# Where VectorE does three things of the last block: a normalisation, a final addition with its statistics, and one wait of GpSimd

## The chip, the cores and the metric

The kernel is one program on one core of a Trainium2 chip. The core has five engines that run their own instruction lists and meet through semaphores: TensorE (PE in the profile; its weight loads are PEld), VectorE (DVE), ScalarE (ACT), GpSimd (POOL) and SyncE (SP), which issues the DMAs. The metric is the time of the program on the device in microseconds; the times below are of one kernel executed three times.

## The reference

Input is a tensor of 8 sequences x 512 tokens x 256 channels. Two layers of a larger model are applied (an attention with a small gating network, a mixture of experts with slots; then a retention-like attention). The last block, which the change touches, is a local attention transformer with two layers:

```python
def _layer(x, wqkv, qs, ksc, wo, lg, lb, w1, b1, w2, b2):
    h = shift_token(x)                      # half of the channels come from the token before
    q, k, v = to_heads(split(h @ wqkv))     # 8 heads of 64
    q, k = rotary_xpos(l2norm(q) * qs, l2norm(k) * ksc)
    x = x + local_attention(q, k, v) @ wo   # windows of 128 tokens, own and previous one
    h = shift_token(x)
    h = (h - h.mean(-1)) / sqrt(h.var(-1) + 1e-05) * lg + lb
    a, g = split(h @ w1 + b1)
    x = x + (a * gelu(g)) @ w2 + b2
```

Behind the second layer the block's input is added again and the sum is normalised over the channels; that is the output.

## The kernel before, in words

All eight sequences stay in on-chip memory. The last block is one software pipeline of 75 slots (`SLOTS4` = 76, counted from 1). A slot takes one tile of 128 tokens of one sequence through each stage of the attention: 64 tiles (8 sequences x 4 tiles x 2 layers). The MLP work of a whole sequence (`m` = 0 to 15: eight sequences, two layers; m = 8 to 15 are the second layer) is cut in pieces and dealt over the slots by the table `PARTS_MLP`: MLP m begins in slot 4m + 7, and every slot has four parts. In the code `r` or `slot - 4m - 7` counts from there.

Each engine has its own function for a slot, and the order of its lines is the order of the engine's queue. The pieces that matter here:

- **gate and lin** (TensorE line 2046 for 128x512 and 2050 for the last piece of 64 rows): two halves of the first MLP product, six pieces each. ScalarE turns a gate with Gelu (line 2157), VectorE adds the bias to a lin and multiplies the two (line 2324, semaphore `m_hid`).
- **hT** (line 2037): transposes of the normalised rows `hn`; they wait for `m_norm`.
- **down** (line 2024): the second product; VectorE adds it to x in pairs (line 2307, `m_xw`).
- **scores** (line 1949), four banks s0 to s3 in two groups of 16 matmuls; VectorE takes row maxima (line 2231) and so frees the banks (`t_max`).
- **weights** (line 1964), w0 to w3: transposes of the probabilities; VectorE copies w0 and w2 out (line 2284, `t_pTd`), ScalarE w1 and w3 (line 2137).
- **normalise** (helper line 2604, four instructions, one a tile): subtracts the mean and multiplies by the reciprocal root. It is called on `hn` (`vector4_shifted`, sets `m_norm`) and on the finished x.
- **statistics** (helper lines 2589 and 2592, four of each), and the reciprocal root on GpSimd (lines 2597 and 2599).
- **final addition** (line 2335): x plus the reloaded input `again`, for m = 8 to 14; m = 15 has its own ending, `vector4_finish`.
- **bias** on GpSimd (line 2412): adds b_2 to x, 1024 values a partition.

Four banks of the accumulator memory (3, 4, 6, 7) go round among the kinds q, k, lin, gate, hT, s, w and down, in the order in which the program uses them; before a use, `emptied4` waits until the use four places earlier has been read. In slot 44 the order is q, k, lin 5, s0, s1, s2, s3, lin 4, hT 0, w0 to w3; in slot 45 it ends with down, w0, w1, w2, w3, gate 0, gate 1.

```python
place = self.ring4.place[kind, m, index] - 4
kind, m, index = self.ring4.uses[place]
w.wait_ge(*{... "w": ("t_pTa" if index % 2 else "t_pTd", 2 * m + index // 2 + 1),
    ... "lin": ("m_hid", 6 * m + LIN_AT[index % len(LIN_AT)] + 1)}[kind])
```

Of the kernel before, what the change touches and what calls it, by code (L numbers as in the profile page):

```python
# [7 lines left out]
ALU = mybir.AluOpType  # L8
# [3 lines left out]
SEQS, TOKENS, CH = 8, 512, 256  # L12
TILES = TOKENS // P
# [4 lines left out]
def split(ap, *sizes):  # L18
    names = "abcd"[:len(sizes)]
    return ap.rearrange(f"p ({' '.join(names)}) -> p {' '.join(names)}", **dict(zip(names, sizes)))  # L20
# [8 lines left out]
def repeated(ap, count):  # L29
    return ap.unsqueeze(1).to_broadcast([ap.shape[0], count] + list(ap.shape[1:]))  # L30
# [1712 lines left out]
TILES4, MLPS = LAYERS * LAYER, LAYERS * SEQS  # L1743
MLP_FIRST, MLP_STEP = 7, 4
# [14 lines left out]
def mlp_pieces(slot, part):  # L1759

    found = []
    for since, kind, index in PARTS_MLP[(slot - MLP_FIRST) % MLP_STEP][part - 1]:
        m = (slot - MLP_FIRST - since) // MLP_STEP
        if m == MLPS - 1 and kind in ("shift", "hT"):
            continue
        if 0 <= m < (SEQS if kind == "back" else MLPS):
            found.append((m, kind, index))
    last = slot - MLP_STEP * (MLPS - 1) - MLP_FIRST
    if (last, part) == (2, 2):
        found[1:1] = [(MLPS - 1, "hT", 0), (MLPS - 1, "hT", 1)]  # L1770
    return found + [(MLPS - 1, kind, index) for kind, index in PARTS_LAST.get((last, part), ())]
# [12 lines left out]
class Block4:  # L1784
# [501 lines left out]
    def vector4_mlp(self, e, w, slot, part):  # L2286
        s, S, own = self.s, self.S, self.own1
        for m in range(MLPS):
            if m == MLPS - 1 and slot == MLP_STEP * m + MLP_FIRST + 1 and part == 3:
                self.vector4_shifted(e, w, m)  # L2290
        if part == 1:
            for m in range(SEQS, MLPS - 1):
                if slot == MLP_STEP * m + MLP_FIRST + 7:
                    w.wait_ge("f_rstd", m - SEQS + 1)
                    self.normalise(e, self.norm4[1], self.x_nat[:, m - SEQS], s["f_norm"])
        for m, kind, index in mlp_pieces(slot, part):
            l, b = divmod(m, SEQS)
            if kind == "down" and m == MLPS - 1:
                self.vector4_finish(e, w, m, index)
                continue  # L2300
            if kind == "down":
                if index % 2:
                    pair = index // 2
                    x = self.x_nat[:, b, 2 * pair:2 * pair + 2]
                    w.wait_ge("m_w2", 4 * m + index + 1)
                    w.wait_ge("m_bias", m + 1)
                    e.tensor_tensor(x, x, split(self.bank4("down", m, 2 * pair), 2, CH), ALU.add).then_inc(s["m_xw"], 1)
                continue
            if kind == "shift":
                w.wait_ge("m_half", 2 * m + 2)  # L2310
                self.stats_of(e, w, "m_shifted", [32 * (m + 1)] * TILES, self.norm4[0], split(self.hn, TILES, CH), s["m_stat"])
                continue
            bank = self.bank4(kind, m, index)
            if kind == "back" and not index:
                w.wait_ge("m_back0", m + 1)
                e.tensor_copy(self.xT[:, b, 0, 1:], bank).then_inc(s["m_yTd"], 1)
            elif kind == "hT" and not index:
                w.wait_ge("m_hp", 2 * m + 1)
                w.wait_ge("l_late", 16)
                e.tensor_scalar(self.hT[:, 0], bank, S(f"l_g{l}")[:, 0:1], S(f"l_b{l}")[:, 0:1], ALU.mult, ALU.add).then_inc(s["m_hTd"], 1)  # L2320
            elif kind == "lin":
                w.wait_ge("m_lin", 6 * m + LIN_AT[index] + 1)
                w.wait_ge("m_gelu", 6 * m + index + 1)
                e.scalar_tensor_tensor(self.hidden[index], bank[:, 0:self.hidden[index].shape[1]], split(S(f"b_1{l}"), 2, HID_TILES)[:, 0, index:index + 1], self.hidden[index],  # L2324
                                       ALU.add, ALU.mult).then_inc(s["m_hid"], 1)

        for m in range(MLPS - 1):
            b = m - SEQS
            if part == 1 and slot == MLP_STEP * m + MLP_FIRST + 1:
                self.vector4_shifted(e, w, m)  # L2330
            elif part == 4 and b >= 0 and slot == MLP_STEP * m + MLP_FIRST + 6:
                x = self.x_nat[:, b]
                w.wait_ge("m_xw", 2 * m + 2)
                w.wait_ge("x%d" % b, 48)
                e.tensor_tensor(x, x, split(self.again, TILES, CH), ALU.add).then_inc(s["f_add"], 1)
                self.stats_of(e, w, "f_add", [b + 1] * TILES, self.norm4[1], x, s["f_stat"])

    def vector4_shifted(self, e, w, m):
        w.wait_ge("m_rstd", m + 1)
        self.normalise(e, self.norm4[0], split(self.hn, TILES, CH), self.s["m_norm"])  # L2340

    def vector4_finish(self, e, w, m, t):

# [49 lines left out]
    def gpsimd4_mlp(self, e, w, slot):  # L2393
        s = self.s
        for m in range(MLPS):
            l, b = divmod(m, SEQS)
            r = slot - MLP_STEP * m - MLP_FIRST
            x = self.x_nat[:, b]
            if r == 0:
                if m:  # L2400
                    w.wait_ge("m_hp", 2 * m)
                e.memset(self.hn[0:1, P:CH], 0.0).then_inc(s["m_half"], 1)
                w.wait_ge("t_x", 4 * m + 4)
                e.tensor_copy(split(self.hn, TILES, CH)[:, :, 0:P], x[:, :, 0:P]).then_inc(s["m_half"], 1)
                w.wait_ge("m_stat", m + 1)
                self.rsqrt(e, w, self.norm4[0], s["m_rstd"])
            elif r == 1:
                w.wait_ge("m_shifted", 32 * (m + 1))
                w.wait_ge("m_half", 2 * m + 2)
                w.wait_ge("m_norm", m + 1)  # L2410
                w.wait_ge("l_late", 16)
                e.tensor_tensor(x, x, repeated(self.S(f"b_2{l}"), TILES), ALU.add).then_inc(s["m_bias"], 1)
            elif r == 6 and m == MLPS - 1:
                small, own = self.norm4[1], self.ownp1
                w.wait_ge("x%d" % b, 48)
                w.wait_ge("m_bias", m + 1)
                e.tensor_tensor(x, x, split(self.again, TILES, CH), ALU.add).then_inc(s["m_bias"], 1)
                for t in range(TILES):
                    w.wait_ge("f_stat", SEQS + t)
                    e.tensor_scalar(small[:, 36 + t:37 + t], split(small[:, 24:32], TILES, 2)[:, t, 1:2], EPS, None, ALU.add).then_inc(own.up(), 1)  # L2420
                    w.wait_ge(own.sem, own.n)
                    e.tensor_tensor(small[:, 32 + t:33 + t], small[:, 36 + t:37 + t], self.half[:, 0:1], ALU.pow).then_inc(s["f_rstd"], 1)
            elif r == 6 and l:
                w.wait_ge("f_stat", b + 1)
                self.rsqrt(e, w, self.norm4[1], s["f_rstd"])
# [65 lines left out]
class Program(Block1, Block2, Block3, Block4):  # L2491
# [41 lines left out]
    def S(self, name):  # L2533
        group, at, n = self.small_at[name]
        return self.pieces[group][:, at:at + n]
# [254 lines left out]
```

## Time and profile before

| | us |
|---|---|
| median of three executions | 2354.67 |
| lowest, highest | 2353.15, 2357.87 |
| the profiled execution | 2357.87 |
| its span in the profile | 2356.1 |
| TensorE busy | 2254.7 (96% of the span) |
| VectorE busy | 1639.4 (70%) |
| ScalarE busy | 1254.6 (53%) |
| GpSimd busy | 731.8 (31%) |

The profile comes from one of the three executions, the slowest. Its engines' rows give a start in us from the beginning of the span, a duration, the engine, the line of the kernel, the operation, and shapes as written and read. A bracket behind a row tells how long the engine had been idle and what released it. Ends of matmuls are modelled, so that starts are safer to read than ends. The last block fills the time from about 1046 us to the end.

### The profile page before, as it was taken

Reading aid. Unit: us, or ns where it says so; the run is one execution under the profiler, and the core shown is the slowest. Engines: PE = TensorE matmul, PEld = TensorE weight load, DVE = VectorE, ACT = ScalarE, POOL = GpSimd, SP = SyncE. Lnnn points to the kernel's source line nnn. Section 1 sums busy time; section 2 is a strip of 40 time slices with the busy share of each in tenths; the row PEclk is TensorE's granted clock in tenths of the full one; section 3 lists DMA queues with packets and bytes.
Section 4 is the critical chain, followed back from the end, with each engine's and each line's share of the span. In section 5 each row is a group of like instructions: output and inputs, shape, how many; then the busy total and the mean of one; then the engine's idle time right before and its main releaser. Section 6 shows DMA issues by size and latency. Waiting matters only on the chain.

```text
span 2356.1 us, 42487 instructions
## 1 busy us (share of the span) xinstructions
PE 2254.7 (96%) x16306; PEld 1322.2 (56%) x16306; DVE 1639.4 (70%) x4252; ACT 1254.6 (53%) x2823; POOL 731.8 (31%) x730
## 2 busy tenths in 40 slices
PE   8999999999898989988899999999999999999998
PEld 3333333333632867765566666666666666666665
DVE  6788888886510846667876777677767777787764
ACT  4666666665221532237666556556665666566640
POOL 3343233321020411134433333343333333333321
PEclk7999999999998999999999999999999999999999
DMA  7444333334279020000000000000001000000001
GB/s 237 144 148 118 118 118 114 117 105 164 94 321 396 2 90 19 19 28 21 6 6 6 1 6 6 6 1 32 15 5 53 6 15 22 13 14 23 21 23 39
DMA packets 68617, 158.44 MB, mean 67 GB/s; under 512 B 6256, under 2 KB 49120, under 8 KB 63936
## 3 DMA queue, kind: packets, MB, share of 16 engines
q1 hardware_dynamic: 65856, 146.55, 17.5%
q0 software_dynamic: 2560, 9.18, 1.7%
q8 instruction: 130, 2.13, 0.4%
q14 instruction: 71, 0.58, 0.1%
HBM read 116.39 MB, written 35.13 MB: 64 GB/s over the span
## 4 chain that ended last, share of the span: by engine, by line
PE 74%; DVE 15%; ACT 4%; DMA 3%; issue 2%; POOL 1%; SPq 0%; POOLq 0%; DVEq 0%; ACTq 0%
PE banks L2046 10%; PE banks L2024 7%; PE banks L1905 6%; PE banks L1919 5%; PE banks L232 5%; PE banks L272 4%; PE banks L245 4%; PE banks L2006 3%; PE banks L1949 3%; PE banks L1964 3%; DVE arena L481 2%; DVE arena L2589 2%; PE banks L1931 2%; DMA arena<-in_e_Wg 2%; PE banks L1428 1%
## 5 line engine op out<-in xcount | busy, mean ns | idle before, releaser
L481 DVE TENSOR_REDUCE arena<-banks 128x1 f32<-128x512 f32 x512 | 323.4, 681 | 72.1 <-PE banks L232 72.0
L393 ACT ACTIVATE arena<-banks 128x512 f32<-128x512 f32 x512 | 280.2, 595 | 146.3 <-PE banks L245 144.2
L2046 PE MATMUL banks<-arena 128*128 128x512 f32 x640 | 293.2, 594 | 1.0 <-DVE arena L2231 1.0
L2128 ACT ACTIVATE arena<-arena 128x256 f32<-128x256 f32 (+1 forms) x512 | 286.5, 562 | 5.0 <-DVE arena L2237 4.5
L2384 POOL TENSOR_TENSOR arena<-arena 128x512 f32<-128x512 f32 x128 | 162.7, 1271 | 380.0 <-DVE arena L2268 380.0
L1905 PE MATMUL banks<-arena 128*128 128x512 f32 x512 | 241.5, 594 | 2.8 <-DVE arena L2268 2.8
L232 PE MATMUL banks<-arena 96*128 96x512 bf16 x512 | 204.8, 403 | 17.5 <-DVE arena L481 14.3
L245 PE MATMUL banks<-arena 128*128 128x512 bf16 x512 | 195.0, 387 | 2.8 <-ACT arena L393 2.2
L2380 POOL TENSOR_TENSOR arena<-arena 128x16 f32<-128x16 f32 x64 | 189.4, 2959 | 5.3
L2100 ACT ACTIVATE arena<-arena 128x256 f32<-128x256 f32 (+1 forms) x256 | 102.1, 471 | 163.2 <-DVE arena L2213 163.2
L2046 PEld LDWEIGHTS banks<-arena 128*128 128x128 f32 x640 | 115.5, 190 | 126.7 <-issue 116.5
L2024 PE MATMUL banks<-arena 128*128 128x256 f32 x768 | 171.1, 379 | 1.9 <-DVE arena L2324 1.9
L2231 DVE CUSTOM_DVE_ANT_0 arena<-banks,arena 128x256 f32<-128x256 f32 (+1 forms) x512 | 168.7, 385 | 3.5 <-PE banks L1949 3.5
L2024 PEld LDWEIGHTS banks<-arena 128*128 128x128 f32 x768 | 144.5, 190 | 28.0 <-issue 6.2
L232 PEld LDWEIGHTS banks<-arena 96*128 96x128 bf16 x512 | 50.5, 99 | 185.3 <-DVE arena L481 115.3
L1905 PEld LDWEIGHTS banks<-arena 128*128 128x128 f32 x512 | 91.5, 190 | 86.9 <-issue 81.3
L272 PE MATMUL banks<-arena 128*32 128x512 f32 x1024 | 137.3, 609 | 1.8 <-ACT arena L393 1.6
L2120 ACT ACTIVATE arena<-banks 128x512 f32<-128x512 f32 x64 | 38.2, 597 | 180.1 <-PE banks L1919 180.1
L2276 DVE TENSOR_TENSOR arena<-arena 128x512 f32<-128x512 f32 x64 | 81.9, 1279 | 73.5 <-POOL arena L2384 73.5
L1919 PE MATMUL banks<-arena 128*128 128x512 f32 x256 | 126.6, 617 | 0.3 <-ACT arena L2078 0.3
L2006 PE MATMUL banks<-arena 128*128 128x256 f32 x512 | 121.2, 380 | 0.0
L1964 PE MATMUL banks<-arena 128*128 128x128 f32 x896 | 119.7, 272 | 0.5 <-DVE arena L2231 0.3
(302 smaller groups left out, 4238.1 us busy)
## 6 DMA issues: line engine op xcount, KB each, us to landing
arena<-in_e_W SPq DMA_DIRECT2D x16, 2048.0 KB, 16.2
arena<-stacks SPq DMA_DIRECT2D x64, 384.0 KB, 4.5
arena<-in_e_Wg SPq DMA_DIRECT2D x8, 2048.0 KB, 17.8
stacks<-arena SPq DMA_DIRECT2D x32, 384.0 KB, 2.5
stacks<-arena SPq DMA_DIRECT2D x32, 256.0 KB, 2.8
arena<-dens POOLq DMA_DIRECT2D x32, 256.0 KB, 4.6
arena<-in_xT SPq DMA_DIRECT2D x8, 512.0 KB, 7.9
stacks<-arena SPq DMA_DIRECT2D x32, 128.0 KB, 2.5
```

The lines of the kernel that those rows point to most:

```text
L232: e.matmul(self.psum[:, k % 3], stack[0:STACK, 0, j, t * P:(t + 1) * P], stack[0:STACK, 1, j, :], start=True, stop=True).then_inc(s["a_max ...
L245: e.matmul(self.psum[:, self.exp_bank1(k)], stack[:, 1, j, t * P:(t + 1) * P], stack[:, 0, j, :], start=True, stop=True).then_inc(s["a_exp ...
L272: i = e.matmul(bank[32 * j:32 * j + 32, :], v[:, t, at:at + 32], ex[:, j], start=t == 0, stop=t == TILES - 1, skip_group_check=True)
L393: e.activation(ex[:, j], self.psum[:, self.exp_bank1(k)], ACT.Exp).then_inc(s["a_e"], 1)
L481: e.tensor_reduce(split(self.maxima[n % 2][:, 0:16], TILES, UNIT)[:, t, j:j + 1], self.psum[:, k % 3], AX.X, ALU.max, negate=True).then_in ...
L1905: k = e.matmul(self.psum[:, side], self.xT[:, b, c, at:at + P], self.wqkv4[:, c, side], start=c == 0, stop=c == 1)
L1919: k = e.matmul(self.psum[:, 2], self.xT[:, b, c, at:at + P], self.wqkv4[:, c, 2], start=c == 0, stop=c == 1)
L1964: k = e.transpose(bank[:, hh, n], pr[:, 2 * pair + hh, n * P:(n + 1) * P], self.ident)
L2006: k = e.matmul(self.psum[:, 2, 0:CH], self.o4[0][:, pair * P:(pair + 1) * P], self.wo4[:, pair], start=pair == 0, stop=pair == 3)
L2024: i = e.matmul(bank[:, t % 2 * CH:(t % 2 + 1) * CH], self.hidden[k][:, at:at + P], self.w2[:, k + t // 2 if last else k], start=k == 0, st ...
L2046: i = e.matmul(bank, weights[:, c], self.hT[:, c], start=c == 0, stop=c == 1)
L2128: k = e.activation(pr[:, h, at:], pr[:, h, at:], ACT.Exp, bias=mx[:, h:h + 1], scale=rn[:, h:h + 1], accum_out=den[:, h:h + 1])
```

## The change

Three things are moved or taken out; nothing is computed differently.

```diff
@@ vector4_mlp
         for m in range(MLPS):
-            if m == MLPS - 1 and slot == MLP_STEP * m + MLP_FIRST + 1 and part == 3:
-                self.vector4_shifted(e, w, m)
+            if slot == MLP_STEP * m + MLP_FIRST + 1 and part == (3 if m == MLPS - 1 else 1):
+                w.wait_ge("m_rstd", m + 1)
+                self.normalise(e, self.norm4[0], split(self.hn, TILES, CH), s["m_norm"])
...
                     e.tensor_tensor(x, x, split(self.bank4("down", m, 2 * pair), 2, CH), ALU.add).then_inc(s["m_xw"], 1)
+                if index == 3 and l:
+                    x = self.x_nat[:, b]
+                    w.wait_ge("m_xw", 2 * m + 2)
+                    w.wait_ge("x%d" % b, 48)
+                    e.tensor_tensor(x, x, split(self.again, TILES, CH), ALU.add).then_inc(s["f_add"], 1)
+                    self.stats_of(e, w, "f_add", [b + 1] * TILES, self.norm4[1], x, s["f_stat"])
                 continue
...
-        for m in range(MLPS - 1):
-            b = m - SEQS
-            if part == 1 and slot == MLP_STEP * m + MLP_FIRST + 1:
-                self.vector4_shifted(e, w, m)
-            elif part == 4 and b >= 0 and slot == MLP_STEP * m + MLP_FIRST + 6:
-                x = self.x_nat[:, b]
-                w.wait_ge("m_xw", 2 * m + 2)
-                w.wait_ge("x%d" % b, 48)
-                e.tensor_tensor(x, x, split(self.again, TILES, CH), ALU.add).then_inc(s["f_add"], 1)
-                self.stats_of(e, w, "f_add", [b + 1] * TILES, self.norm4[1], x, s["f_stat"])
-
-    def vector4_shifted(self, e, w, m):
-        w.wait_ge("m_rstd", m + 1)
-        self.normalise(e, self.norm4[0], split(self.hn, TILES, CH), self.s["m_norm"])
@@ gpsimd4_mlp, r == 1
                 w.wait_ge("m_shifted", 32 * (m + 1))
                 w.wait_ge("m_half", 2 * m + 2)
-                w.wait_ge("m_norm", m + 1)
                 w.wait_ge("l_late", 16)
```

`normalise` on `hn` stands in the same slot and part as before, but ahead of the pieces of that part and not behind them. For m = 15 it stays. The order of TensorE, ScalarE and SyncE is the same in both kernels.

VectorE in slot 4m + 8, m = 9, before. Semaphores appear under the name that an earlier block gave them: a_rstd is `m_rstd`. L2324 is the product with lin 5, L2604 is `normalise`, L2242 joins the two halves of the attention output:

```order
L2254 TENSOR_REDUCE arena<-arena 128x8 [waits s_exp] x2
L2324 SCALAR_TENSOR_TENSOR arena<-banks,arena 128x256 [waits m_gelu,m_lin]
L2604 TENSOR_SCALAR arena<-arena 128x256 [waits a_rstd]
L2604 TENSOR_SCALAR arena<-arena 128x256 x3
L2242 TENSOR_TENSOR arena<-arena,banks 128x512 [waits c_cp]
```

The same place in the changed kernel, where L2595 is `normalise` and L2331 the product:

```order
L2254 TENSOR_REDUCE arena<-arena 128x8 [waits s_exp] x2
L2595 TENSOR_SCALAR arena<-arena 128x256 [waits a_rstd]
L2595 TENSOR_SCALAR arena<-arena 128x256 x3
L2331 SCALAR_TENSOR_TENSOR arena<-banks,arena 128x256 [waits m_gelu,m_lin]
L2242 TENSOR_TENSOR arena<-arena,banks 128x512 [waits c_cp]
```

The four instructions of `normalise` have changed places with the product.

VectorE in slot 45 (m = 8, r = 6) before, from the addition of the last down pair (L2307) on; L2265 and L2268 rotate queries and keys, L2335 is the final addition, L2213 belongs to the next slot:

```order
L2307 TENSOR_TENSOR arena<-arena,banks 128x512 [waits m_w2]
L2284 COPY arena<-banks 128x512 [waits c_av,c_turn]
L2265 TENSOR_TENSOR arena<-banks,arena 128x512 [waits x_back]
L2268 TENSOR_TENSOR arena<-banks,arena 128x8x32 x2
L2198 TENSOR_TENSOR arena<-arena,banks 128x256 [waits q_mm]
L2284 COPY arena<-banks 128x512 [waits c_turn]
L2265 TENSOR_TENSOR arena<-banks,arena 128x512
L2268 TENSOR_TENSOR arena<-banks,arena 128x8x32 x2
L2276 TENSOR_TENSOR arena<-arena 128x512 [waits t_rn,t_qa]
L2335 TENSOR_TENSOR arena<-arena 128x1024 [waits x0,s_gath]
L2589 BN_STATS arena<-arena 128x6 [waits a_m]
L2589 BN_STATS arena<-arena 128x6 x3
```

The same place now, from the same addition (here L2308) on; L2313 is the final addition, and s_gath is `m_xw`:

```order
L2308 TENSOR_TENSOR arena<-arena,banks 128x512 [waits m_w2]
L2313 TENSOR_TENSOR arena<-arena 128x1024 [waits x0,s_gath]
L2580 BN_STATS arena<-arena 128x6 [waits a_m]
L2580 BN_STATS arena<-arena 128x6 x3
L2583 BN_AGGR arena<-arena 128x2 [waits a_dve]
L2583 BN_AGGR arena<-arena 128x2 x3
L2284 COPY arena<-banks 128x512 [waits c_av,c_turn]
L2265 TENSOR_TENSOR arena<-banks,arena 128x512 [waits x_back]
L2268 TENSOR_TENSOR arena<-banks,arena 128x8x32 x2
```

Nine instructions have moved ahead of the copy of w0 and of both rotations. The same holds for m = 9 to 13; for m = 14 nothing stands between L2307 and the addition in either kernel.

GpSimd in slot 64 (m = 14), before, between two reciprocal roots (L2597, L2599); a_norm is `m_norm`:

```order
L2599 TENSOR_TENSOR arena<-arena 128x4 [waits a_pool]
L2412 TENSOR_TENSOR arena<-arena 128x1024 [waits a_norm,m_half,m_shifted]
L2597 TENSOR_SCALAR arena<-arena 128x4 [waits a_prep]
```

And in the changed kernel:

```order
L2590 TENSOR_TENSOR arena<-arena 128x4 [waits a_pool]
L2403 TENSOR_TENSOR arena<-arena 128x1024 [waits m_half,m_shifted]
L2588 TENSOR_SCALAR arena<-arena 128x4 [waits a_prep]
```

The order is the same, one wait is gone.

## Rows read from the trace of the kernel before

**Rows 1.** Busy time by engine in a stretch, with granted clock.

```profile
core 0: us, PE busy (x) PEld busy (x) DVE busy (x) ACT busy (x) POOL busy (x), PEclk, DMA share, GB/s
2000.00:2100.00 100.00, 99.67 (x793) 64.58 (x795) 78.34 (x232) 60.38 (x149) 36.59 (x31) 1.00 0.05 16
```

**Rows 2.** TensorE's waits from 1200 us on: total, times, longest.

```profile
PE banks L1949 <- DVE arena L2324: 2.3, 13, 0.3
PE banks L2024 <- DVE arena L2324: 1.9, 2, 0.9
PE banks L1949 <- ACT arena L2107: 1.5, 1, 1.5
PE banks L2046 <- DVE arena L2231: 1.0, 1, 1.0
PE banks L1931 <- DVE arena L2276: 0.4, 1, 0.4
```

**Rows 3.** Timeline of slot 44: start, duration, engine, line, operation.

```profile
1863.24 0.48 DVE L2324 SCALAR_TENSOR_TENSOR arena<-banks,arena 128x256 f32<-128x256 f32 x1
...
1863.63 1.37 DVE L2604 TENSOR_SCALAR arena<-arena 128x256 f32<-128x256 f32 x4
...
1863.77 0.88 PE L1949 MATMUL banks<-arena 64*64 64x192 f32 x16 [0.16 <-DVE arena L2324]
...
1864.92 0.68 DVE L2242 TENSOR_TENSOR arena<-arena,banks 128x512 f32<-128x512 f32 x1
```

**Rows 4.** Timeline of slot 45 and the start of slot 46.

```profile
1891.68 0.69 DVE L2307 TENSOR_TENSOR arena<-arena,banks 128x512 f32<-128x512 f32 x1 [4.54 <-PE banks L2024]
1892.28 0.68 DVE L2284 COPY arena<-banks 128x512 f32<-128x512 f32 x1
...
1894.96 3.60 PE L2046 MATMUL banks<-arena 128*128 128x512 f32 x8
...
1898.05 0.69 DVE L2276 TENSOR_TENSOR arena<-arena 128x512 f32<-128x512 f32 x1 [1.38 <-POOL arena L2384]
...
1898.66 1.22 DVE L2335 TENSOR_TENSOR arena<-arena 128x1024 f32<-128x1024 f32 x1
...
1901.64 0.17 DVE L2213 RECIPROCAL arena<-arena 128x8 f32<-128x8 f32 x1
...
1902.26 0.60 PE L1931 MATMUL banks<-arena 128*128 128x128 f32 x4
```

**Rows 5.** VectorE's timeline in slot 69 (m = 14).

```profile
2317.26 0.69 DVE L2307 TENSOR_TENSOR arena<-arena,banks 128x512 f32<-128x512 f32 x1 [2.22 <-PE banks L2024]
2317.98 1.22 DVE L2335 TENSOR_TENSOR arena<-arena 128x1024 f32<-128x1024 f32 x1
```

**Rows 6.** One of GpSimd's waits from 1200 us on: total, times, longest.

```profile
POOL arena L2412 <- DVE arena L2604: 4.5, 2, 2.9
```

**Rows 7.** Timeline in slot 70, VectorE and GpSimd.

```profile
2322.54 3.54 DVE L2604 TENSOR_SCALAR arena<-arena 128x256 f32<-128x256 f32 x4 [1.47 <-POOL arena L2599]
2322.93 2.35 POOL L2417 TENSOR_TENSOR arena<-arena 128x1024 f32<-128x1024 f32 x1 [0.43 <-DMA arena<-kept_x]
```

**Rows 8.** Timeline around slot 64, VectorE and GpSimd.

```profile
2254.74 1.04 POOL L2599 TENSOR_TENSOR arena<-arena 128x4 f32<-128x4 f32 x1
...
2255.11 1.14 DVE L2217 TENSOR_SCALAR arena<-arena 128x256 f32<-128x256 f32 x4
...
2257.16 1.38 DVE L2604 TENSOR_SCALAR arena<-arena 128x256 f32<-128x256 f32 x4
```

**Rows 9.** Timeline of slot 68, GpSimd and TensorE.

```profile
2309.61 1.04 POOL L2599 TENSOR_TENSOR arena<-arena 128x4 f32<-128x4 f32 x1
...
2313.59 1.04 PE L2037 MATMUL banks<-arena 128*128 128x128 f32 x8
```

**Rows 10.** A wait of TensorE ahead of the key turn, timeline.

```profile
1165.86 0.63 PE L1931 MATMUL banks<-arena 128*128 128x128 f32 x4 [2.29 <-DVE arena L2276]
```

**Rows 11.** Busy time and granted clock in two stretches, columns as in rows 1.

```profile
1160.00:1170.00 10.00, 7.71 (x108) 5.49 (x108) 7.52 (x14) 5.39 (x12) 4.33 (x4) 0.83 0.00 1
...
2255.00:2260.00 5.00, 2.55 (x77) 2.00 (x70) 4.96 (x17) 2.67 (x6) 2.07 (x2) 1.00 0.01 3
```

## The prediction, made before the changed kernel ran

> **What bounds the kernel now.** I read the busy share by stretches first. In the last block (1200 us to the end) TensorE is busy 99.67 of every 100 us at a granted clock of 1.00 [rows 1]. The reader is to see that nothing else comes near (VectorE 78.34), and that any microsecond added to a wait of TensorE there is a microsecond of the kernel unless another wait swallows it. Next came TensorE's waits over the same block [rows 2]: 7.1 us in all. There is almost nothing to win, and almost nothing that could swallow a new stall. The first line is the one that matters: 13 times TensorE waits for line 2324, a "lin" product of VectorE, 0.18 us on average. All 13 are the same place, once every four slots. Then I read the timeline at one such place [rows 3], at one place where the final addition stands [rows 4], and at slots 64 and 68, where GpSimd has no other work [rows 8, 9].
>
> **Part 1: `normalise` ahead of the last lin piece (slots 4m+8, m = 1 to 14).** In slot 44 VectorE multiplies lin 5 from 1863.24 for 0.48 us, and 0.05 us after its end TensorE's second group of 16 score matmuls starts, having idled 0.16 us [rows 3]. That is no accident of timing: four banks go round, the order of uses in slot 44 is q, k, lin 5, s0, s1, s2, s3, so s3 takes the bank of lin 5. In the changed order four `normalise` instructions stand ahead of lin 5. They take 1.37 us; from the first of them to line 2242 behind them is 1864.92 - 1863.63 = 1.29 us. So lin 5 ends 1.29 us later and TensorE's second score group starts 1.29 us later. What is behind `normalise` on VectorE (line 2242, the row maxima) starts when it did before, since the two only change places; it is therefore no cover. Nobody gains: the first reader of the normalised rows on TensorE comes later in the slot, and no line of its waits names `normalise` [rows 2]. Bounds for a place: below nothing by the present 0.16 us if the stall went altogether, above 1.37 us. I take 1.29. 13 places x 1.29 = 16.8 us. The fourteenth (slot 64) is counted in part 3, for m = 0 there is no lin 5 in that slot, and m = 15 keeps its order.
>
> **Part 2: final addition and statistics moved from part 4 to part 2 (m = 8 to 13).** In slot 45 VectorE now does line 2307, then 2284 (the copy of transposed weights w0), and only at 1898.66 the addition [rows 4]. The block of addition, four statistics and four aggregations fills 1898.66 to 1901.64 = 2.98 us. It moves to right behind line 2307. There it must also wait for the end of 2307 rather than follow it in the pipe: in the tail, where the two do stand together, the distance is 2317.98 - 2317.26 = 0.72 us [rows 5]. So 2284 starts at 1891.68 + 0.72 + 2.98 = 1895.38 and ends at 1896.06. By the order of banks (..., w0, w1, w2, w3, gate 0) the gate 0 matmul takes w0's bank, and it starts at 1894.96 now [rows 4]. It will start at 1896.06 + 0.05 = 1896.11, a stall of 1.15 us. The later waits of that chain survive: the key turn at 1902.26 needs line 2276, which ends at 1898.74 and would end 3.1 us later, at 1901.8; TensorE arrives later by 1.15 us besides. Behind the block the next reciprocal (line 2213) moves by about 0.1 us. Bounds: nothing if gate 0 were covered, 2.98 us if nothing covered the block. There are six places (m = 8 to 13); for m = 14 the addition already follows line 2307 directly [rows 5], so nothing moves in the tail. 6 x 1.15 = 6.9 us. The wait for the reloaded input and SP's queue only come earlier: the next reload is released by the addition itself.
>
> **Part 3: GpSimd's bias addition without the wait for `normalise`.** In slots up to 63 GpSimd still has the query and key sums of the slot ahead of it, and its wait is long satisfied: from 1200 us on only two bias additions waited for `normalise` [rows 6]. These, in slots 64 and 68, will now start at once behind the reciprocal root. There it meets VectorE. What that costs the tail shows: line 2417, 2.35 us on GpSimd, starts inside a `normalise` and the four instructions last 3.54 us instead of 1.38 [rows 7, 8]. VectorE stands still for nearly the whole GpSimd instruction. The Trainium skill, "SBUF — State Buffer", section "Who interferes with whom", says that a tensor_scalar of VectorE in a two-port mode and a GpSimd instruction shut each other out for a whole instruction, whoever comes first. By that rule, the trace agrees; it would make each meeting cost one GpSimd instruction.
> In slot 64 the root ends at 2255.78; VectorE's line 2217 runs from 2255.11 to 2256.25 [rows 8], so its last instruction, starting near 2255.9, waits until 2255.85 + 2.35 = 2258.2. Everything behind it, the key copy for the scores and the row maxima that free a bank for line 2046, comes 2.3 us late, and TensorE already waits for both here (1.5 and 1.0 us, rows 2). Price 2.3 us; the swap is inside it, since the row maxima keep their place. Bounds: 0 (no meeting) and 2.3 + 1.7 (the clock, below).
> In slot 68 the root ends at 2310.65; the addition takes 2.36 us, until 2313.01; `normalise` then 1.37 us, until 2314.4. TensorE wants the result at 2313.59 [rows 9]: 0.8 us. Bounds 0 and 2.2. The bias result is wanted by nobody earlier.
>
> **The sum.** 16.8 + 6.9 + 2.3 + 0.8 = 26.8 us. The profiled execution took 2357.87 us (span 2356.1 and 1.8 around it) and would become 2384.7. It was the slowest of the three; for the median of 2354.67 I forecast 2381.5 us, +1.1%.
>
> **Rivals.**
> A: only the swap costs. Gate 0 is covered after all, because TensorE's loads of weights run ahead and the copy in question is freed in another way. For it: no wait of that kind is in rows 2. Against it: the bank order, and only 1894.96 - 1892.96 = 2.0 us of slack against 3.1 us of delay. 2381.5 - 6.9 = 2374.6 us. Chance 10%.
> B: only the added blocks cost and lin 5's lateness is swallowed. It would need a later wait of TensorE in the same period of at least 1.3 us. Rows 2 have none. 2364.7 us. Chance 4%.
> C: the clock. After a wait of 2.29 us at 1165.86 the granted clock over 10 us was 0.83 [rows 10, 11], a loss of 0.17 x 10 = 1.7 us. If each of the 20 stalls did that: 2381.5 + 34 = 2415.5 us. Against it: in 2255 to 2260, with waits of 1.5 and 1.0 us, it stayed at 1.00 [rows 11], and my new stalls in the steady part are 1.15 and 1.45 us. Chance 4%; that slot 64 alone drops it (idle there could grow to 1.5 + 2.3 us) is in my range. The Trainium skill, "TensorE: Matmul & The Clock Gate", section "HAM oscillation — how this bites in real kernels", tells of a kernel whose array slowed again at each wait; by that rule C would hold, and the row with clock 1.00 speaks against it here.
> D: not slower. VectorE would have to reach lin 5 earlier against TensorE by 1.29 + 0.16 us a period, so that the swap fills an idle time. That happens if VectorE's sequence is not tied to TensorE and runs ahead as TensorE falls back: the point is whether VectorE waits for TensorE anywhere in the four slots. If it did not, the first stall would buy off all the others, the 2.3 us of present waits would go too, and the copy in slot 45 would be on time: 2354.7 + 1.3 - 2.3 = 2353.7 us plus slots 64 and 68 if they meet. Against it: line 2307 in rows 4 sat idle 4.54 us for TensorE, once a period, which ties VectorE to it anew. Chance 4%.
>
> **How the numbers follow.** My forecast 78%, A 10%, B 4%, C 4%, D 4%. The forecast's own spread: swap 1.2 to 1.37 a place, block 1.0 to 1.3, slots 64 and 68 together 0 to 6 us, and 1.5 us for the median before. With A's value inside, the range is 2374 to 2388 us. A change of under 0.2% (4.7 us) can't be told from none here. Faster 2%, within 4%, slower 94%: D is split over the first two, everything else is above 2359.4.
>
> **What would show it.** TensorE's wait for the lin product would grow from 0.16 to 1.45 us, 13 times (19 us in all); a new line would stand in its waits, gate 0 (line 2046) for the weights copy (line 2284), six times 1.1 us; the bias addition would start before 2256 + the shift in slot 64 with a 2217 or `normalise` of about 2.5 us beside it; the period of four slots would grow by 1.3 us in the first layer and by 2.4 in the second; the clock would stay at 1.00. Should the wait on lin stay under 0.5 us, part 1 is wrong; should no gate line appear, A.

## The result, and the profile after

| | before | changed |
|---|---|---|
| median, us (4 executions each, same chip) | 2354.43 | 2385.81 |
| lowest, highest | 2353.15, 2357.87 | 2384.15, 2388.07 |
| profiled execution, and its span | 2357.87, 2356.1 | 2384.17, 2382.4 |

The changed kernel is slower: ratio 1.0132, 95% interval 1.0114 to 1.0149, that is 27 to 35 us. The forecast was 2381.5 us, range 2374 to 2388.

TensorE's waits in the last block of the changed kernel, as in [rows 2]; L2331 is the lin product, L2284 the copy of transposed weights, L2595 `normalise`:

```profile
PE banks L1949 <- DVE arena L2331: 19.8, 14, 1.6
PE banks L2046 <- DVE arena L2284: 5.9, 6, 1.0
PE banks L1949 <- issue: 3.2, 1, 3.2
PE banks L2024 <- DVE arena L2331: 1.9, 2, 0.9
PE banks L1931 <- DVE arena L2276: 0.4, 1, 0.4
PE banks L2037 <- DVE arena L2595: 0.4, 1, 0.4
```

They have grown from 7.1 to 31.6 us. The first line is the one of [rows 2] with 2.3 us; the second did not exist; the third and the last are slots 64 and 68. "issue" names no releaser; in the timeline this wait of 3.15 us ends 0.1 us behind the end of VectorE's key copy (line 2175, 2278.13 us for 0.68 us). The changed place in slot 44, which answers to [rows 3]:

```profile
1870.10 0.83 PE L1949 MATMUL banks<-arena 64*64 64x192 f32 x16
1870.57 1.38 DVE L2595 TENSOR_SCALAR arena<-arena 128x256 f32<-128x256 f32 x4
...
1871.86 0.48 DVE L2331 SCALAR_TENSOR_TENSOR arena<-banks,arena 128x256 f32<-128x256 f32 x1
...
1872.39 0.88 PE L1949 MATMUL banks<-arena 64*64 64x192 f32 x16 [1.46 <-DVE arena L2331]
...
1873.20 1.12 PE L1919 MATMUL banks<-arena 128*128 128x512 f32 x2
```

`normalise` runs, then the product, and 0.05 us after it the second score group, with 1.46 us idle ahead of it in place of 0.16. And slot 45, which answers to [rows 4]:

```profile
1900.25 0.69 DVE L2308 TENSOR_TENSOR arena<-arena,banks 128x512 f32<-128x512 f32 x1 [4.54 <-PE banks L2024]
...
1900.98 1.23 DVE L2313 TENSOR_TENSOR arena<-arena 128x1024 f32<-128x1024 f32 x1
...
1903.98 0.66 DVE L2284 COPY arena<-banks 128x512 f32<-128x512 f32 x1
...
1904.69 3.70 PE L2046 MATMUL banks<-arena 128*128 128x512 f32 x8 [0.99 <-DVE arena L2284]
```

From L2308 to the copy it is now 3.73 us, where it was 0.60, and gate 0 stands 0.99 us.

**A ledger by starts.** Up to slot 11 the kernels here differ only in slot 8 (`normalise` and the bias addition of m = 0), and yet this part takes a different time in each execution: line 1919 (the matmuls of the values, once a slot) of slot 11 starts at 1205.53 us before, at 1202.89 in the changed kernel, and anywhere from 1198.76 to 1213.17 in the profiled executions below. So I compare from that start to the start of the last matmuls (line 2024). Shift against the kernel before, the one at slot 11 taken off:

| stretch | changed kernel, us | per place |
|---|---|---|
| slots 12 to 63, 13 swaps | 16.2 | 1.25 |
| slots 45 to 61, 5 additions | 6.3 | 1.26 |
| slot 64 | 4.6 | |
| slot 65, the sixth addition | 1.3 | |
| slot 68 | 0.6 | |
| slot 11 to the end | 28.9 | |

The lines are rounded one by one. This holds to about 0.05 us a place: line 1919 of slot 12 starts at 1224.59 before and at 1223.25 after, so that the shift goes from -2.64 to -1.34. In the span 2.6 of the 28.9 us are hidden, because this execution reached slot 11 earlier. The medians say 31.4 us, and their interval holds 28.9.

### The profile page after: what moved, and what is told of

Its sections match the earlier page's. It is cut to its first block, busy times and chain, and to the rows that moved or that the text cites. A ratio compares the mean times of both kernels' runs of the same rounds, so it can differ in the third digit from the quotient of the medians.

```text
span 2382.4 us, 42437 instructions
## 1 busy us (share of the span) xinstructions
PE 2254.7 (95%) x16257; PEld 1324.2 (56%) x16306; DVE 1641.0 (69%) x4252; ACT 1253.6 (53%) x2823; POOL 733.3 (31%) x730
## 4 chain that ended last, share of the span: by engine, by line
PE 71%; DVE 17%; DMA 4%; ACT 4%; issue 3%; POOL 2%; SPq 0%; another core or an unknown queue 0%; POOLq 0%; DVEq 0%; ACTq 0%
PE banks L2046 9%; PE banks L2024 7%; PE banks L1905 6%; PE banks L1919 5%; PE banks L232 4%; PE banks L272 4%; PE banks L245 3%; PE banks L2006 3%; PE banks L1949 3%; PE banks L1964 2%; DVE arena L481 2%; DVE arena L2580 2%; PE banks L1931 2%; DMA arena<-in_e_Wg 1%; PE banks L1428 1%
## 5 line engine op out<-in xcount | busy, mean ns | idle before, releaser
L245 PE MATMUL banks<-arena 128*128 128x512 bf16 x463 | 175.9, 385 | 3.0 <-ACT arena L393 2.2
L2367 POOL TENSOR_SCALAR arena<-arena 128x16 f32<-128x16 f32 x64 | 17.9, 280 | 339.9 <-DVE arena L2254 339.8
```

Source lines behind the costliest of these rows:

```text
L245: e.matmul(self.psum[:, self.exp_bank1(k)], stack[:, 1, j, t * P:(t + 1) * P], stack[:, 0, j, :], start=True, stop=True).then_inc(s["a_exp ...
```

## The experiments

All are edits of the kernel before, unless said otherwise, and all compute the same output. "From slot 11" is the measure of the ledger. Medians are against the kernel before on the same chip; they scatter by some us for the reason given.

### The parts alone

The first has only `normalise` moved:

```diff
-            if m == MLPS - 1 and slot == MLP_STEP * m + MLP_FIRST + 1 and part == 3:
+            if slot == MLP_STEP * m + MLP_FIRST + 1 and part == (3 if m == MLPS - 1 else 1):
                 self.vector4_shifted(e, w, m)
...
-            if part == 1 and slot == MLP_STEP * m + MLP_FIRST + 1:
-                self.vector4_shifted(e, w, m)
```

> The kernel before with part 1 alone: normalise ahead of the lin 5 product for m = 1 to 14. My theory (lin 5's bank is wanted by the fourth score bank, s3): TensorE's wait for the product in 13 places is 1.46 us and the start of line 1919 shifts by 1.3 us each time, about 16.5 us by slot 63; slot 64 adds under 0.5 us, since the row maxima there keep their place. About 2371 us. Rival (the loss comes from VectorE as a whole being later, so only the three edits together give it): under 10 us.

Median 2375.76 us, ratio 1.0079 (1.0059 to 1.0099); from slot 11 16.2 us longer, all of it in the 13 places, nothing in slot 64. The waits name the product 14 times, 19.4 us. The rival falls.

The second has only the addition moved; `vector4_again` is the addition with its statistics, taken out of part 4:

```diff
                     e.tensor_tensor(x, x, ...bank4("down", m, 2 * pair)...).then_inc(s["m_xw"], 1)
+                if index == 3 and l:
+                    self.vector4_again(e, w, m, b)
...
```

> The kernel before with part 2 alone: final addition and statistics directly behind the last down pair, m = 8 to 13. My theory: gate 0 waits for the copy of w0, 1.0 us idle, 1.2 us of shift in each of six places, 7.5 us in all, about 2362 us; nothing moves before slot 45. Rival (gate 0 stalls only because the swap had already moved things): no change.

Median 2364.61 us, ratio 1.0032 (1.0018 to 1.0046); from slot 11 7.6 us: nothing up to slot 45, then 1.26 a place. TensorE's wait of line 2046 for line 2284 is there six times, 5.9 us, as in the changed kernel. The stall does not need the swap.

The third has only GpSimd's wait taken out:

```diff
-                w.wait_ge("m_norm", m + 1)
```

> The kernel before with part 3 alone: GpSimd's bias addition without its wait for normalise. Theory with the clock: in slot 64 VectorE stands for one GpSimd instruction (2.2 us), TensorE idles over 3 us at a stretch, its granted clock falls there, and the slot costs 4.6 us in place of 2.3; slot 68 costs 0.6: together 5.2 us, about 2360 us. Rival (the extra 2.3 us in slot 64 of the changed kernel came from the swap, with lin 5 behind normalise): 2.3 + 0.6 = 2.9 us.

Median 2359.47 us, ratio 1.0007 (0.9997 to 1.0018), not told from no change; from slot 11 2.6 us, of which slot 64 has 2.03 and slot 68 0.6. That is near the rival's number. Yet the idle time of over 3 us that my clock theory asks for is there, and so is the slow clock. Slot 64 of this kernel, timeline (L2411 is the bias addition), and then the busy time with the granted clock ahead of the last two columns:

```profile
2253.75 3.23 DVE L2217 TENSOR_SCALAR arena<-arena 128x256 f32<-128x256 f32 x4
...
2254.39 2.44 POOL L2411 TENSOR_TENSOR arena<-arena 128x1024 f32<-128x1024 f32 x1
...
2256.91 0.68 DVE L2175 COPY arena<-banks 128x512 f32<-128x512 f32 x1
...
2257.68 2.84 PE L1949 MATMUL banks<-arena 64*64 64x192 f32 x32 [3.15 <-issue]
...
2260.60 1.98 PE L2046 MATMUL banks<-arena 128*128 128x512 f32 x4
```

```profile
2257.60:2260.50 2.90, 2.82 (x32) 1.97 (x32) 2.90 (x11) 0.00 (x0) 0.00 (x0) 0.52 0.00 0
2260.50:2262.40 1.90, 1.82 (x7) 0.82 (x5) 1.86 (x14) 0.93 (x3) 0.00 (x0) 1.00 0.00 0
```

The meeting is as [rows 7] had it: the four instructions of line 2217 take 3.23 us in place of 1.14 [rows 8]. The clock goes to its lower level (1.2 GHz) for the scores, which take 2.84 us, and is up again (2.4 GHz) when line 2046 starts. The scores have time there, since line 2046 waits for row maxima that VectorE makes at its own pace. So the slow clock cost nothing, and the 2.0 us are the meeting alone; a kernel below (lin 5 early, on the changed one) has the same meeting with the clock at 1.00 throughout, and its slot 64 costs 2.04 us.

The three parts add to 16.2 + 7.6 + 2.6 = 26.4 us; the changed kernel has 28.9. The missing 2.5 us lie in slot 64.

### Is it the bank of w0?

Here the addition and its statistics stand one instruction later than in the changed kernel: behind the copy of w0, and still ahead of both rotations.

```diff
             if c is not None:
                 self.vector4_weights(e, w, c, 0)
+            m, r = divmod(n - MLP_FIRST - 6, MLP_STEP)
+            if r == 0 and SEQS <= m < MLPS - 1:
+                self.vector4_again(e, w, m, m - SEQS)
             if a is not None:
                 self.vector4_rotate(e, w, a, 0)
...
```

> The kernel before with the final addition and its statistics moved to part 2 of the slot, but one instruction later than in the changed kernel: behind the copy of w0 (line 2284) and ahead of both rotations. My theory (the bank of w0): the whole block of 3 us still stands ahead of rotations and key scaling, but gate 0 finds its bank free, and the time is that of the kernel before within 1 us. Rival (VectorE's delay of rotations and of what follows is what counts): still 5 to 8 us slower.

From slot 11 0.05 us longer, though the additions still stand ahead of both rotations. Median 2359.99 us, ratio 1.0015 (1.0001 to 1.0029), which by itself would allow a small loss; its executions reach from 2354.38 to 2364.87 us, and the profiled one, with 2364.86, had lost 6.95 us before slot 11 and nothing behind it. Slot 45, where L2287 is the copy and L2339 the addition:

```profile
1899.23 0.68 DVE L2287 COPY arena<-banks 128x512 f32<-128x512 f32 x1
...
1899.83 1.21 DVE L2339 TENSOR_TENSOR arena<-arena 128x1024 f32<-128x1024 f32 x1
...
1901.91 3.60 PE L2046 MATMUL banks<-arena 128*128 128x512 f32 x8
```

Gate 0 has no idle time. One copy of 0.68 us on the other side of the block is worth 7.6 us; the three other delays of 3 us (both rotations, the second copy) are worth nothing.

### The dose: two of four instructions

Two of the four instructions of `normalise` go ahead of lin 5, two stay behind it.

```diff
+            elif m < MLPS - 1 and slot == MLP_STEP * m + MLP_FIRST + 1 and part == 1:
+                w.wait_ge("m_rstd", m + 1)
+                self.normalise_tiles(e, (0, 1))
...
             if part == 1 and slot == MLP_STEP * m + MLP_FIRST + 1:
-                self.vector4_shifted(e, w, m)
+                self.normalise_tiles(e, (2, 3)).then_inc(s["m_norm"], 1)
```

> The kernel before with two of the four normalise instructions ahead of lin 5 and two behind it. My theory (the stall is as long as what stands ahead of lin 5): half of 1.3 us a place, 13 x 0.65 = 8.5 us, about 2363 us; the idle time ahead of the second score group is 0.8 us. Rival (a threshold: any delay of lin 5 costs a fixed step, for example because TensorE's queue has to be filled anew): the full 16 us.

Median 2366.27 us, ratio 1.0052 (1.0038 to 1.0065); from slot 11 7.9 us, 0.61 a place, and 0.81 us idle in the record of slot 44:

```profile
1868.96 0.83 PE L1949 MATMUL banks<-arena 64*64 64x192 f32 x16
...
1870.61 0.88 PE L1949 MATMUL banks<-arena 64*64 64x192 f32 x16 [0.81 <-DVE arena L2327]
1871.42 1.98 PE L1919 MATMUL banks<-arena 128*128 128x512 f32 x4
```

Half of the instructions give half of the loss: proportional, no step.

### Lin 5 ahead of the lengths

The product with lin 5 becomes a function of its own and is called one place earlier; this is done to the kernel before and to the changed one:

```diff
+            self.vector4_lin5(e, w, n)
             if a is not None:
                 self.vector4_lengths(e, w, a)
...
-            elif kind == "lin":
+            elif kind == "lin" and (index < 5 or part != 1):
```

> The kernel before with the lin 5 product ahead of line 2254, nothing else. My theory: the 13 waits of 0.16 us vanish and nothing else moves: 2 us faster, about 2352.4 us, at the edge of what can be measured; in the trace the line of TensorE's waits for the product ahead of the scores is gone. Rival (line 2254, later by 0.4 us, delays GpSimd's roots and the next turn): no gain or slower by some us.

Median 2350.3 us, ratio 0.9985 (0.9975 to 0.9995). From slot 11 it is 5.0 us shorter and not 2. The scores of slot 44 in this kernel (L2349 is lin 5, L2255 the lengths):

```profile
1855.79 0.48 DVE L2349 SCALAR_TENSOR_TENSOR arena<-banks,arena 128x256 f32<-128x256 f32 x1 [0.33 <-PE banks L2050]
...
1856.34 1.28 DVE L2255 TENSOR_REDUCE arena<-arena 128x8 f32<-128x512 f32 x2
...
1857.06 1.48 PE L1949 MATMUL banks<-arena 64*64 64x192 f32 x32
...
1858.48 1.98 PE L1919 MATMUL banks<-arena 128*128 128x512 f32 x4
```

The product falls into the time in which VectorE waited for ScalarE, and from the scores to line 1919 it is 1.42 us. The kernel before has these two starts in slot 44:

```profile
1862.77 0.83 PE L1949 MATMUL banks<-arena 64*64 64x192 f32 x16
...
1864.58 1.98 PE L1919 MATMUL banks<-arena 128*128 128x512 f32 x4
```

The same distance is 1864.58 - 1862.77 = 1.81 us there, 2.46 with two `normalise` ahead, and 3.10 in the changed kernel (1870.10 to 1873.20). The steps are 0.39, 0.65 and 0.64 us. So the kernel before lost 0.39 us in each place where its record shows 0.16 idle [rows 3]: the idle time is counted from a modelled end, the starts are not.

> The kernel before with lin 5 ahead of line 2254, once more, for a closer interval: the trace of its first run was 5.0 us shorter from slot 11 to the end (0.38 us in each of 13 places, where the record showed an idle time of 0.16). Theory (the record's idle time is measured from a modelled end of the matmuls and is too small; the true stall was 0.34 to 0.38): again 4.5 to 5.5 us in the trace, ratio near 0.998. Rival (the first run's 5 us were chance): 2 us.

From slot 11 again 5.0 us shorter; median 2349.34 us against 2355.16, ratio 0.9982 (0.9967 to 0.9997). The theory stands. This version beats both kernels, the kernel before by 4.4 and 5.8 us of the median in its two runs.

> The changed kernel with the lin 5 product taken out of the MLP pieces and put ahead of line 2254 (the lengths), where VectorE idles 0.87 us for ScalarE; normalise stays where the change put it. My theory (only the lateness of lin 5 costs): all 13 stalls are gone, the present 0.16 us too, and about 7.5 + 5 - 2 = 10.5 us over the kernel before are left, about 2365 us. Rival (normalise ahead of the attention's additions costs by itself): still over 20 us slower than before.

Median 2359.86 us, ratio 1.0025 (1.0016 to 1.0035); from slot 11 5.2 us over before. All swap stalls are gone with `normalise` left where the change put it, which takes 28.9 - 5.2 = 23.7 us off the changed kernel: 16.2 + 5.0 in the 13 places and 2.5 in slot 64. The rival falls; my 10.5 us were too high by the 3 us more that the early product gains, and by slot 64, which here costs 2.0.

### Slot 64: the meeting and the clock

> The kernel before without GpSimd's wait for normalise, and the bias addition in four instructions of one tile (128x256) in place of one of 128x1024. If VectorE and GpSimd shut each other out for one instruction at a time, VectorE loses 0.6 us a meeting in slot 64 and not 2.35; TensorE's idle time stays near 2 us, the clock stays at 1.00, and slots 64 and 68 together cost 1 to 2 us. Rival (the two share the time evenly while both work, however the work is cut): as with the long instruction, 5 us.

The wait is out, and the bias addition is `for t in range(TILES): e.tensor_tensor(x[:, t], x[:, t], b_2, ALU.add)`. Median 2353.37 us, ratio 1.0001 (0.9989 to 1.0012); from slot 11 1.2 us, of which slot 64 has 0.94 and slot 68 0.2. Line 2217 takes 1.61 us in place of 3.23. VectorE loses short instructions, not a share of the time.

> Parts 1 and 3 together, without part 2. In the traces of the parts alone, slot 64 costs nothing (swap) and 2.0 us (wait removed), in the changed kernel 4.6 us. Theory (the clock): with both, TensorE idles twice in slot 64, over 3 us and again 0.8 us for lin 5, and the granted clock is down when the bank for line 2046 comes free, so that its four matmuls take 3.8 us in place of 2.0: slot 64 costs 4.6 us here too, and from slot 11 to the end the trace is 16.1 + 4.6 + 0.5 = 21.2 us longer. Rival (the extra time needs part 2, whose late copies shift the slots behind): 16.1 + 2.6 = 18.7 us.

Median 2375.71 us, ratio 1.0097 (1.0077 to 1.0117). From slot 11 19.3 us: slot 64 costs 2.5 us. My 21.2 was wrong, the rival's 18.7 nearer. But the clock was down here too, only sooner.

> The changed kernel with GpSimd's bias addition cut in four instructions of one tile. Theory: VectorE loses two short meetings in slot 64 and not one long one, TensorE's longest idle time there stays under 2.5 us, the clock stays at 1.00, and slot 64 costs about 1 to 1.5 us in place of 4.6: from slot 11 to the end 28.9 - 3.5 = 25.4 us over before. Rival (the clock falls because of the swap's idle time, whatever the length of the bias instruction): above 27.5 us.

Median 2379.03 us, ratio 1.0109 (1.0087 to 1.0130); from slot 11 26.8 us, slot 64 2.9 us. That is between my 25.4 and the rival's 27.5: the meeting shrank, but the clock fell all the same, after idle times of only 1.54 and 1.67 us.

Slot 64 in the changed kernel, timeline, then busy time and granted clock:

```profile
2275.61 2.45 POOL L2403 TENSOR_TENSOR arena<-arena 128x1024 f32<-128x1024 f32 x1
...
2278.91 0.88 PE L1949 MATMUL banks<-arena 64*64 64x192 f32 x16 [3.15 <-issue]
...
2280.55 1.56 PE L1949 MATMUL banks<-arena 64*64 64x192 f32 x16 [0.76 <-DVE arena L2331]
...
2282.04 3.78 PE L2046 MATMUL banks<-arena 128*128 128x512 f32 x4
...
2287.49 1.89 PE L2006 MATMUL banks<-arena 128*128 128x256 f32 x8
```

```profile
2278.90:2280.50 1.60, 0.88 (x16) 0.54 (x16) 1.60 (x6) 0.00 (x0) 0.00 (x0) 0.82 0.00 0
2280.50:2282.00 1.50, 1.45 (x16) 0.80 (x16) 1.50 (x6) 0.00 (x0) 0.00 (x0) 0.50 0.00 0
2282.00:2285.60 3.60, 3.60 (x8) 1.41 (x5) 2.16 (x14) 2.45 (x8) 0.00 (x0) 0.50 0.00 0
2285.60:2287.50 1.90, 1.90 (x14) 1.89 (x13) 1.54 (x3) 0.00 (x0) 0.00 (x0) 0.70 0.00 0
```

The same stretches with parts 1 and 3 alone, and then with the bias by tile:

```profile
2271.90:2273.50 1.60, 1.41 (x16) 0.82 (x16) 1.60 (x6) 0.00 (x0) 0.00 (x0) 0.58 0.00 0
2273.50:2275.00 1.50, 1.41 (x16) 0.80 (x16) 1.50 (x7) 0.00 (x0) 0.00 (x0) 0.50 0.00 0
2275.00:2278.40 3.40, 3.40 (x20) 2.29 (x17) 3.28 (x16) 2.45 (x8) 0.00 (x0) 0.92 0.00 0
```

```profile
2273.10:2275.60 2.50, 0.88 (x16) 0.56 (x16) 2.50 (x6) 0.38 (x1) 1.33 (x2) 1.00 0.00 0
2275.60:2276.90 1.30, 0.88 (x16) 0.51 (x16) 1.30 (x7) 0.00 (x0) 0.00 (x0) 0.95 0.00 0
2276.90:2280.50 3.60, 3.54 (x6) 1.54 (x7) 2.39 (x15) 2.44 (x8) 0.00 (x0) 0.54 0.02 5
```

Line 2046 is the first thing in the slot from which on TensorE is busy without a break. From its start to line 2006 the kernel before and the one without the wait take 3.2 and 3.1 us; with the low clock there it is 5.45 us (changed kernel) and 4.72 us (bias by tile). In the changed kernel the rest of the slot's cost, up to the start of line 2046, is 2.3 us (from the first attention matmul, line 1990, 7.85 us, before 5.55). Of these 2.1 are the meeting: VectorE's row maxima start 6.04 us behind line 2217, before 3.94, and in the kernel without the wait 6.03. The other 0.2 us lie between the first row maximum and line 2046 (1.03 us, in those two kernels 0.82), behind a second score group that began late and ran at the low clock. So 4.6 = 2.1 for the meeting + 2.5 with the clock. With parts 1 and 3 the low clock covered mostly the scores, and line 2046 to line 2006 took 3.4 us. The kernel with the early lin 5 on the changed one had 3.16 us idle and stayed at 1.00 throughout.

The changed kernel and the one with parts 1 and 3 have the same starts in this slot: the scores 1.70 us and line 2046 2.30 us later than before. Yet the clock fell 1.0 us behind the start of the scores in the first and 0.2 us in the second. So the waits of the slot alone do not decide it, and no run shows what part 2 has to do with it. Each of these is one profiled execution.

## Why the prediction was right

The range held the time and the sign and the mechanism were as forecast. Step by step, from slot 11:

| step | forecast | measured |
|---|---|---|
| swap, 13 places | 16.8 (1.29 each) | 16.2 (1.25 each) |
| addition, 6 places | 6.9 (1.15 each) | 7.6 (1.26 each) |
| slot 64 | 2.3 | 4.6; alone 2.0 |
| slot 68 | 0.8 | 0.6; alone 0.6 |
| sum | 26.8 | 28.9 |

The first two terms were off by -0.6 and +0.7 us, which cancel by luck; what is left of the difference is slot 64 (+2.3) and slot 68 (-0.2).

- **Part 1.** Lin 5's bank for s3 was the right cover to name. The stall in the record is 1.46 us against the 1.45 of the forecast. The dose and the removal of the stall show it from both sides. What I had wrong is what the kernel before already lost there: 0.39 us and not 0.16, by the starts.
- **Part 2.** Right in place and nearly in size; one copy decides it. The shift of 1.26 us is again larger than the recorded idle time of 0.99. The later waits of that chain, which I had left with 0.4 us of room, did survive.
- **Part 3.** The meeting of VectorE and GpSimd in slot 64 is 2.1 us in the changed kernel, against 2.3 in the forecast. The term that was mis-sized is slot 64 as a whole: I kept the clock outside the sum and only in the bound (2.3 + 1.7 = 4.0 us), expected it to stay at 1.00, and it came with 2.5 us, so that the slot's 4.6 us lie above that bound. That the time for it was to be had from [rows 11] at all rested on one dip.
- **Rivals.** A falls: the wait for the copy is there six times. B falls by the first experiment. C was right in one slot of twenty: in the 19 other places the clock stayed at 1.00 and the shifts are 1.25 to 1.26 us each. The kernel that the prediction cites for C from the Trainium skill ("TensorE: Matmul & The Clock Gate", "HAM oscillation — how this bites in real kernels") waits longer at each stop than the 1.46 us of these stalls, so C did not follow from it. D falls; the early product shows what it would have taken, and VectorE can't get there by itself.
- The median rose by 31.4 us and not 28.9. The difference is within the interval, and the profiled pair differs by 26.3 us of span, on the other side. The start of slot 11 moved by up to 14 us between executions. Nearly all of that arises ahead of the last block: its first matmul (line 1905) starts at 1023.59 us before and between 1015.85 and 1031.14 in the other traces. What moves it was not looked into.

Still open is what sets the moment at which the clock falls. In the changed kernel, with idle times of 3.15 and 0.76 us, it fell 1.0 us behind the end of the first; with parts 1 and 3, 0.2 us behind it; without the wait it was down already when the scores started; with 1.54 and 1.67 us it fell 1.1 us behind both; with 3.16 us and lin 5 early not at all.

## What to carry to other kernels

Where one engine is busy 99.7% of the time, look not at how much work an edit moves but at which buffer each moved instruction frees and who takes it next: here one 0.48 us product and one 0.68 us copy decided 24 of 29 us, and moving the product a place earlier, into a wait that VectorE had anyway, made a kernel that beats both. Count stalls by the distance between starts of the same two instructions in two kernels; a recorded idle time behind matmuls can be half of the truth. And split a run at the first changed instruction before comparing: noise ahead of it was larger here than a whole part of the change.

## What the runs showed of the hardware

- A tensor_scalar of VectorE on on-chip memory stood still for nearly a whole addition of GpSimd: the four of line 2217 took 1.14 us without a meeting, 3.23 us beside one addition of 2.44 us, and 1.61 us beside four of some 0.75 us. The Trainium skill ("SBUF — State Buffer", "Who interferes with whom") says that the two lock each other out for whole instructions; for VectorE's side, the traces agree, and they add that cutting the long instruction is a remedy: 2.6 us became 1.2.
- The granted clock fell to 0.50 for 6.8 us in one slot of the changed kernel (from the four stretches above) and made four matmuls of 128x512 take 3.78 us in place of 1.98. The fall in the kernel without the wait (0.52 over the 2.90 us of the scores) cost nothing, since line 2046 had to wait for VectorE's row maxima anyway.
- Idle times read behind matmuls were too short by 0.2 to 0.3 us: 0.16 recorded for 0.39 lost, 0.99 recorded for 1.26 lost, 1.46 recorded for 1.68 lost (3.10 - 1.42).
